# Attention unit and sine layer: the own term moved into the exponentials' diagonal, row sums by feature, values projected first, sine added in PSUM

## The reference

```python
# part 1: heads of 64, causal mask, 2 x 16 heads, n = 1024
attn = softmax(q @ k.T)                       # masked above the diagonal
out  = attn @ v
adj  = clip(attn + eye(n), 0, 1);  deg = adj.sum(-1)
feats = v
for l in range(2):
    h = feats @ gnn_w[l] + gnn_b[l]
    feats = gelu((adj @ h) / deg + feats)
out = out + feats @ lin_w + lin_b
return layer_norm(out @ Wo, gamma_out)
...
# part 2: hidden of 512 features
hidden = x @ W1 + b1
q = hidden + quantum_phase * w_imag * sin(theta + 0.1 * hidden) * 0.1
return relu(q) @ W2 + b2
```

## Time and profile before

| | before |
|---|---|
| median of 3 runs | 2194.48 us (2192.84 to 2197.96) |
| the profiled execution | 2188.13 us, span 2186.3 us |
| PE / PE weight loads busy | 1659.2 us (76%) / 1028.0 us (47%) |
| DVE / ACT / POOL busy | 1128.1 (52%) / 679.5 (31%) / 785.5 us (36%) |
| attention unit, 28 to 1133 us | PE busy 1045.5 us |
| sine layer, 1165 to 1243 us | PE busy 43.1 us, DVE 73.2 us |

### The profile page before, as it was taken

One profiled execution on the slowest core, in us unless ns is written; L12 is line 12 of the kernel. 1 busy time (PEld: TensorE's weight loads), 2 busy tenths in 40 slices (PEclk: granted clock), 3 DMA queues, 4 the chain that ended last, 5 costly groups with the idle time before them and its releaser, 6 DMA issues. The chain is left out here.

```text
span 2186.3 us, 26512 instructions
## 1 busy us (share of the span) xinstructions
PE 1659.2 (76%) x9289; PEld 1028.0 (47%) x9289; DVE 1128.1 (52%) x2512; ACT 679.5 (31%) x990; POOL 785.5 (36%) x511
## 2 busy tenths in 40 slices
PE   3999999999989999999965576955209464767647
PEld 1555655555655556555642345624106211222437
DVE  4334443443444444444448823557703468999615
ACT  1333334433233333334303321322003154544212
POOL 0444345544244443455400031000152105899424
PEclk9899999999999999999886675977559676899759
DMA  1000000000000000000000000000511211212051
GB/s 42 6 6 6 5 5 5 5 0 5 6 1 5 5 5 5 5 5 0 1 1 11 0 6 3 18 12 2 178 46 33 57 31 57 78 67 78 3 153 67
DMA packets 47610, 55.87 MB, mean 26 GB/s; under 512 B 9296, under 2 KB 35048, under 8 KB 47264
## 3 DMA queue, kind: packets, MB, share of 16 engines
q1 hardware_dynamic: 44624, 48.91, 7.5%
q0 software_dynamic: 2912, 6.02, 0.8%
HBM read 42.75 MB, written 12.15 MB: 25 GB/s over the span
## 5 line engine op out<-in xcount | busy, mean ns | idle before, releaser
L356 POOL TENSOR_TENSOR l0a_acc<-l0a_E 128x1792 f32<-128x1792 f32 x16 | 64.3, 4018 | 448.0 <-ACT l0a_E L428 448.0
L821 DVE SCALAR_TENSOR_TENSOR l0a_scrap<-l0a_ring,main_ident 128x128 f32<-128x128 f32 x256 | 74.5, 291 | 271.7 <-PE l0a_ring L560 267.2
L428 ACT ACTIVATE l0a_E<-l0a_ring 128x1024 f32<-128x1024 f32 x192 | 148.8, 809 | 211.8 <-DVE l0a_scrap L821 210.6
L356 POOL TENSOR_TENSOR l0a_acc<-l0a_acc,l0a_E 128x1536 f32<-128x1536 f32 (+2 forms) x96 | 200.8, 2092 | 21.6 <-ACT l0a_E L428 14.0
L2505 PE MATMUL mx_ysum<-mx_hst,main_ident 128*128 128x512 f32 x256 | 142.6, 693 | 44.0 <-POOL mx_hst L2593 38.5
L2606 POOL TENSOR_TENSOR mx_dBu<-mx_XI,mx_BB 128x1024 f32<-128x1024 f32 x64 | 137.5, 2175 | 88.7 <-DVE mx_XI L2669 88.7
L570 PE MATMUL l0a_agg<-l0a_E,l0a_VH 128*64 128x512 f32 (+3 forms) x768 | 154.5, 510 | 0.0
L570 PE MATMUL l0a_agg<-l0a_E,l0a_F 128*64 128x512 f32 (+3 forms) x768 | 141.3, 496 | 0.0
L2578 ACT ACTIVATE mx_dA<-mx_DT,mx_A 128x512 f32<-128x512 f32 x128 | 87.9, 690 | 98.1 <-DVE mx_hst L2686 98.1
L2505 PEld LDWEIGHTS mx_ysum<-mx_hst,main_ident 128*128 128x128 f32 x256 | 54.1, 220 | 115.9 <-POOL mx_hst L2593 57.5
L162 PE MATMUL n_turned<-main_ident,n_xn 128*128 128x128 f32 x96 | 25.8, 458 | 90.6 <-DVE n_xn L132 90.6
(11 more groups left out here) (483 smaller groups left out, 3701.2 us busy)
## 6 DMA issues: line engine op xcount, KB each, us to landing
mx_BB<-mx_brows SPq DMA_DIRECT2D x32, 512.0 KB, 3.6
me_W<-in_f_w SPq DMA_DIRECT2D x16, 256.0 KB, 9.6
l0a_wp<-in_wqkv SPq DMA_DIRECT2D x16, 192.0 KB, 2.3
moe_Wg<-in_f_wg SPq DMA_DIRECT2D x8, 256.0 KB
moe_Wu<-in_f_wu SPq DMA_DIRECT2D x8, 256.0 KB
moe_Wd<-in_f_wd SPq DMA_DIRECT2D x8, 256.0 KB
moe_Y<-rt_zeros SPq DMA_DIRECT2D x2, 1024.0 KB, 10.3
e_back<-moe_Y SPq DMA_DIRECT2D x8, 256.0 KB, 4.8
```

Source lines behind the costliest of these rows:

```text
L356: pool.tensor_tensor(dst, src, E[:, :, ecol[jt]:ecol[jt] + w], ALU.add).then_inc(acc_done, 1)
L428: act.activation(E[:, :, at:at + n], pair(k % 2)[:, :, 0:n], ACT.Exp).then_inc(exp_done, 1)
L821: dve.scalar_tensor_tensor(scrap[:, :], pair(k % 2)[:, h, 0:P], 1.0, ident[:, :], ALU.mult, ALU.mult, accum_out=eii[:, jt, h:h + 1]).then_ ...
```

## The change

The row sums are no longer 16 products of one column: `row_sums` multiplies 64 columns of ones by E and acc, so each head's sum stands in its 64 feature partitions for 1024 tokens, and ScalarE copies it to `RB` (`keep_sums`). `turn_sums` brings them to the old form by 8 products with `pick2` (two columns). `inverse` takes the reciprocals of RB on VectorE, `attended` multiplies them by U untransposed; both run for unit g - 1 within the score stretch of unit g, and `keep_out` adds the result, so `turn_u` and the product with AO in `mix` go. `set_own` adds (s - e) to the 16 diagonals of E in place, so G and `add_own` go, and the aggregation of F1 waits for it. The values are projected ahead of the row scores instead of between them. ScalarE's FT copies stand behind `gelu1` of the first half and both halves of the values. On VectorE the row maxima come after `out1`. In `tail` 7 of the 8 partial products of the output projection are taken ahead of the last pair (`out_tiles`), all of it into two banks, copied in two pieces. In `l0_ffn` four hidden tiles stay in PSUM; ScalarE writes both the angle and the angle in turns; VectorE takes turns off in five instructions; TensorE adds the sine by a product with a diagonal matrix of the coefficients (`add_sine`), and the relu reads PSUM. Declarations, semaphores and the small phase and coefficient sums are left out below.

```diff
-            def keep_v(u):
-                for c in range(2):
-                    act.wait_ge(vw_ready, u * 2 + (c + 1))
-                    wait(act, t1a_done, u * 2)
-                    v = ring[c][:, :].rearrange("p (a w) -> p a w", w=2 * P)
-                    t = slice(4 * c, 4 * c + 4)
-                    act.activation(VH[:, t, :], v[:, :, 0:P], ACT.Copy).then_inc(v_kept, 1)
-                    act.activation(VW[:, t, :], v[:, :, P:2 * P], ACT.Copy).then_inc(vw_kept, 1)
+            def keep_v(u, c):
+                act.wait_ge(vw_ready, u * 2 + (c + 1))
+                wait(act, t1a_done, u * 2 + (c - 1))
+                v = ring[c][:, :].rearrange("p (a w) -> p a w", w=2 * P)
+                t = slice(4 * c, 4 * c + 4)
+                act.activation(VH[:, t, :], v[:, :, 0:P], ACT.Copy).then_inc(v_kept, 1)
+                act.activation(VW[:, t, :], v[:, :, P:2 * P], ACT.Copy).then_inc(vw_kept, 1)
+
+            def keep_sums(g, c):
+                act.wait_ge(r_ready, g * 2 + (c + 1))
+                act.activation(half(RB, c), (prod, turn)[c][:, :], ACT.Copy).then_inc(r_kept, 1)
+
+            def gelu1(g, c):
+                act.wait_ge(s1_done, g * 2 + (c + 1))
+                act.activation(tiles4(F1, c), heads8(S, c).rearrange("p a w -> p (a w)"), ACT.Gelu).then_inc(gelu1_done, 1)
...
+                        wait(act, at_done, g * 2)
                         act.activation(half(UT, 0), agg[0][:, :], ACT.Copy).then_inc(ut_kept, 1)
+                keep_sums(g, 0)
...
+                if nb is not None:
+                    keep_v(g + 1, 0)
+                gelu1(g, 0)
+                if nb is not None:
+                    keep_v(g + 1, 1)
+                if prev is not None:
+                    keep_ft(g, 0)
+                    keep_ft(g, 1)
+                gelu1(g, 1)
...
+            def row_sums(g, prev, nb, c):
+
+                if c:
+                    if nb is not None:
+                        pe.wait_ge(comp_kept, g + 2)
+                        pe.wait_ge(ft_kept, g * 2 - 2)
+                elif prev is None:
+                    wait(pe, ot_kept, g * 2)
+                else:
+                    pe.wait_ge(s2a_done, g * 2)
+                pe.wait_ge(acc_done, g * 7 + (7 if c else 3))
+                bank = (prod, turn)[c]
+                if c == 0:
+                        pe.matmul(bank[hi(h), 0:P], one[:, :], e_tile(h, 0, 0), start=True, stop=True, skip_group_check=True)
+                    for h in range(2):
+                        mm = pe.matmul(bank[hi(h), P:512], one[:, :], acc[:, h, 0:512 - P], start=True, stop=True,
+                                       skip_group_check=True)
+                    for h in range(2):
+                        mm = pe.matmul(bank[hi(h), :], one[:, :], acc[:, h, 512 - P:SEQ - P], start=True, stop=True,
+                                       skip_group_check=True)
+                mm.then_inc(r_ready, 1)
+
+            def turn_sums(g):
+
+                pe.wait_ge(r_kept, g * 2 + 2)
+                for it in range(ST):
+                    mm = pe.matmul(turn[:, 2 * it:2 * it + 2], RB[:, it * P:(it + 1) * P], pick2[:, :], start=True, stop=True)
+                mm.then_inc(s_ready, 1)
...
                 attend(g, 7)
                 product1(g, 0)
+                turn_sums(g)
                 if nb is not None:
-                    row_scores(u, 0, 1)
-                product1(g, 1)
-                if nb is not None:
-                    row_scores(u, 2)
+                    values(u, nb)
                 if prev is not None:
-                    if nb is not None:
-                        pe.wait_ge(comp_kept, u + 1)
+                    pe.wait_ge(s_read, g + 1)
                     turn_f(g, 0)
                 if nb is not None:
-                    row_scores(u, 3)
+                    row_scores(u, 0)
+                product1(g, 1)
+                if prev is not None:
+                    turn_f(g, 1)
+                if nb is not None:
+                    row_scores(u, 1)
                 if prev is not None:
                     pe.wait_ge(s1a_done, g * 2 + 2)
                     mix(g, 0)
-                    turn_f(g, 1)
-                if nb is not None:
-                    values(u, nb)
+                pe.wait_ge(gelu1_done, g * 2 + 1)
+                pe.wait_ge(own_set, g * 16 + 16)
+                for jt in range(4):
+                    mm = aggregate(F1, jt, 0)
+                    if jt == 1 and nb is not None:
+                        row_scores(u, 2)
+                mm.then_inc(agg2_ready, 1)
                 if prev is not None:
                     mix(g, 1)
-                pe.wait_ge(gelu1_done, g * 2 + 1)
-                for jt in range(4):
-                    aggregate(F1, jt, 0, False)
-                turn_u(g, prev, 0)
-                if nb is not None:
-                    row_scores(u, 4)
-                add_own(g, 0)
                 for jt in range(ST):
+                    if nb is not None and jt in (0, 1, 2, 4, 5):
+                        row_scores(u, {0: 3, 1: 4, 2: 5, 4: 6, 5: 7}[jt])
                     if jt == 4:
                         pe.wait_ge(gelu1_done, g * 2 + 2)
+                    mm = aggregate(F1, jt, 1)
+                    if jt == 1:
                         product2(g, prev, 0)
-                    aggregate(F1, jt, 1, False)
-                    if jt == 1:
-                        turn_u(g, prev, 1)
-                    if nb is not None and jt in (1, 3, 4):
-                        row_scores(u, {1: 5, 3: 6, 4: 7}[jt])
+                mm.then_inc(agg2_ready, 1)
                 if nb is not None:
                     max_rows(u)
-                add_own(g, 1)
+                product2(g, prev, 1)
...
+                b = n // PAIRS - 1
+                pe.wait_ge(u2_kept, n * 2)
+                pe.wait_ge(ot_kept, n * 2 - 2)
+                out_tiles(b, n, 0, PAIRS - 1, 0, 1)
                 turn_f(n, 0)
+                out_tiles(b, n, 0, PAIRS - 1, 2, 3)
                 pe.wait_ge(s2a_done, n * 2)
                 mix(n, 0)
                 turn_f(n, 1)
+                out_tiles(b, n, 0, PAIRS - 1, 4, 5)
                 mix(n, 1)
+                out_tiles(b, n, 0, PAIRS - 1, 6, 7)
...
+            def inverse(n, *tiles):
+                for it in tiles:
+                    t = slice(it * P, (it + 1) * P)
+                    dve.reciprocal(AT[:, t], RB[:, t]).then_inc(inv_done, 1)
+
+            def attended(n, c):
+                dve.wait_ge(inv_done, n * ST - (4 - 4 * c))
+                dve.tensor_tensor(half(AT, c), half(AT, c), half(UT, c), ALU.mult).then_inc(at_done, 1)
+
+            def set_own(g):
+                for jt in range(ST):
+                    for h in range(2):
+                        k = 2 * jt + h
+                        dve.scalar_tensor_tensor(e_tile(h, jt, jt), ident[:, :], small[:, 2, k:k + 1], e_tile(h, jt, jt),
+                                                 ALU.mult, ALU.add).then_inc(own_set, 1)
...
+                if prev is not None:
+                    inverse(g, 0, 1)
                 for jt in range(1, ST):
                     own_score(g, jt)
+                    if prev is not None:
+                        inverse(g, *{1: (2, 3), 2: (4, 5), 3: (6,), 4: (7,)}.get(jt, ()))
+                        if jt in (3, 5):
+                            attended(g, (jt - 3) // 2)
                 u = g + 1
                 more = nb is not None
                 if more:
                     keep_q_lo(u)
+                    keep_k_lo(u)
                 sums(g)
-                if more:
-                    keep_k_lo(u)
                 dve.wait_ge(small_ready, u)
                 scaled(S, g, 0, p1_ready, s1a_done)
+                set_own(g)
+                out1(g, 0)
+                scaled(S, g, 1, p1_ready, s1a_done)
+                out1(g, 1)
                 if more:
-                    row_max(u, 0)
-                out1(g, 0)
-                if more:
-                    row_max(u, 1)
-                scaled(S, g, 1, p1_ready, s1a_done)
+                    row_max(u, 0, 1)
+                if prev is not None:
+                    keep_out(g, prev, 0)
                 if more:
                     row_max(u, 2)
-                out1(g, 1)
+                if prev is not None:
+                    keep_out(g, prev, 1)
                 if more:
-                    row_max(u, 3)
-                if prev is not None:
-                    keep_out(g, prev, 0)
-                    keep_out(g, prev, 1)
-                attended(g, 0)
-                if more:
-                    row_max(u, 4)
-                attended(g, 1)
-                if more:
-                    row_max(u, 5, 6)
+                    row_max(u, 3, 4)
...
+            def angle(n):
                 g, c = items[n]
                 act.wait_ge(hid_ready, n + 1)
-                if n >= 3:
```

(42 more changed lines are left out.)

## The result

The changed kernel takes 2235.98 us (2234.87 to 2239.19) against 2194.07 us (2192.84 to 2197.96) of the kernel before, measured side by side: a ratio of 1.019, 95% interval 1.0173 to 1.0208. It is 41.9 us slower. The forecast was 2248 us, with a range of 2165 to 2305. The profiled execution took 2239.19 us around a span of 2237.2.

The account below looks back on a forecast made before the run. The prediction took TensorE's order of work to bound the attention and VectorE the sine layer. Passes +74, output projection -7 and sine layer -13 gave +54 on 2194.5 us: 2248 us, range 2165 to 2305.

Parts of the forecast that it names:

- The chain, with t = 0 at the last piece of scores: Attention pass: set_own beside GpSimd's T delays out1, gelu and the FT copy; TensorE stands still 6.7 us, until 22.0.
- My 19.5: End of out1(g, 0) in us: 18.2 if T's first half falls in, 20.6 if all does; 19.5 taken.
- The two rivals without sharing: set_own does not meet GpSimd: 2150 us if the clock holds, chance 0.18; 2200 us with clock as forecast, chance 0.17.
- The rest of the pass: From TensorE's return to the next third piece of scores 25.1 us, then 19.0; with clock losses the pass is 68.8.
- The new wait of 0.95 at the third piece: TensorE waits 0.95 us at the third piece of scores, since product2(1) no longer stands between scores 1 and 2.
- my sum of 2.7: Clock loss per pass in us: 1.8 for the fall behind the 6.7 us wait, 0.9 for half of a second.
- +74 us for the passes: Attention: each pass grows by 4.8 us, counted for 15.5 passes; range +26 to +102 us.
- Reciprocals: Score stretch: eight reciprocals on VectorE, 0.95 us each, 7.6 a pass, lie in gaps between own scores and cost nothing.
- the rival with 0.12: Reciprocals share the port with GpSimd's sums too: +7 us a pass, 2356 us; chance 0.12.
- Output projection: Batch tail: 56 of 64 products move ahead of the last mixes into waits; -3.4 us a batch, -7 us in all.
- Sine layer: Items take 3.5 to 3.8 us instead of 4.65; fourteen items at -0.95 give -13 us (-23 to +12).

Follow-up runs that it names:

- ft_first: The kernel of split with ScalarE's copy of the first half of FT ahead of the copies of the second value half; 2152.81 us.
- split: Changed kernel with value and FT copies ahead of both gelu1, and the last eight corrections moved behind the fifth row maximum; 2148.1 us, ratio 0.9778.

## Why the prediction was right, step by step

**The chain, with t = 0 at the last piece of scores, was right.** The sums are ready at 9.2 (9.6), the corrections start at 11.0 (11.5), out1(0) ends at 19.2 (19.5), TensorE goes on at 21.5 (22.0) after 6.90 us (6.7). The two terms on which it rests were measured apart: the corrections 4.29 us alone (4.3 taken, 0.27 each), and 3.3 us more beside T. My 19.5 was a choice between 18.2 and 20.6, since no row told how turns are given; that it came within 0.3 us is in part luck. The trace now tells. The sixteen corrections, one by one:

```profile
507.33 0.68 DVE L868 SCALAR_TENSOR_TENSOR l0a_E<-main_ident,l0a_small,l0a_E 128x128 f32<-128x128 f32 x1
507.93 1.43 DVE L868 SCALAR_TENSOR_TENSOR l0a_E<-main_ident,l0a_small,l0a_E 128x128 f32<-128x128 f32 x1
509.29 1.13 DVE L868 SCALAR_TENSOR_TENSOR l0a_E<-main_ident,l0a_small,l0a_E 128x128 f32<-128x128 f32 x1
510.34 1.42 DVE L868 SCALAR_TENSOR_TENSOR l0a_E<-main_ident,l0a_small,l0a_E 128x128 f32<-128x128 f32 x1
511.68 0.34 DVE L868 SCALAR_TENSOR_TENSOR l0a_E<-main_ident,l0a_small,l0a_E 128x128 f32<-128x128 f32 x1
```

Here the engines take turns by the instruction: each of the first four corrections ends about 0.15 us after one of T's four operations, and the other twelve, with GpSimd at rest, follow at 0.26 us. Four in 4.35 us instead of 1.05 is the 3.3.

The Trainium skill, SBUF — State Buffer, section Terms, has the loser of the port block fully; the traces agree, with 7.58 us beside T, 7.29 beside F1B and VB, and 4.29 beside nothing. The two rivals without sharing had 0.35 between them, and they fell.

**The rest of the pass.** From TensorE's return to the third piece of scores I had 25.1 us and 2.7 for the clock, 27.8; it is 28.1 (517.78 to 545.89), and from there to the next last piece 18.7 (19.0). The new wait of 0.95 at the third piece is there, 0.94 us. The wait before max_rows shrank from 1.31 to 0.5 us and no fall follows it. So the clock falls once a pass, not twice, but for 2.8 us of loss instead of 1.8: my sum of 2.7 was right by luck, through two errors that cancel. The steady pass is 68.3 against 68.8.

**The term that was too large is +74 us for the passes.** I took +4.8 us for 15.5 passes; the traces give +58.9. The ten steady intervals went from 64.0 to 68.1, +4.15 each: 6.5 us less than forecast. The first two of each batch grew by 3.4 on average: 5.6 less. The two eighth units grew by 2.0 and 4.6 and the start shrank by 2.8, so the 1.5 further passes of my count are worth 3.8 us and not 7.2. Most of the miss is thus the growth of a pass, and only 3.4 us is the count. Why the first passes of a batch grow less no run shows.

**Reciprocals.** 0.89 to 0.95 us each and never longer, though GpSimd's sums run beside them: the rival with 0.12 is out. They are hidden (the time is 1.7 us shorter without them). `attended` takes 2.2 us instead of 0.69 for its second half, as the prediction had it wait for GpSimd, and the own score behind it costs nothing. What the prediction didn't say is how full the gaps are by then: doubled, they cost 3.4 us a pass.

**Output projection.** Forecast -3.4 a batch; the tails are 4.7 and 4.8 us shorter, -9.5 in all. The early products by themselves are worth 9.2 and 11.1 a batch, as their kernel showed, and part of that only makes up for the eight reciprocals in the tail, behind which TensorE waits 5.68 us without them.

**Sine layer.** Forecast -13, and measured -8.4 and -8.0. The item is faster than I said, 2.97 us by VectorE (3.5 to 3.8), since the clock is 0.86 in the stage and TensorE's products are not the limit. What I left out is a wait. `add(g)` stands in VectorE's order one item after `down(g)` in TensorE's, ahead of the next item's reduction, and `down` is 32 halves, 3.7 us, behind the item's own products. VectorE waits for it four times:

```profile
DVE main_x L1091 <- PE l0f_outp L1109: 20.0, 4, 7.1
```

```profile
1234.81 0.42 DVE L1069 TENSOR_SCALAR l0f_m<-l0f_m 128x512 f32<-128x512 f32 x1
...
1242.72 0.69 DVE L1091 TENSOR_TENSOR main_x<-l0f_outp,main_x 128x512 f32<-128x512 f32 x1 [4.85 <-PE l0f_outp L1109]
```

Before, the combination of the item before stood there (L1048) and an addition at the same place, 1192.48, waited for nothing. By the windows VectorE has 24.1 us less work in the layer (55.7 instead of 79.8), and it is idle for 24.6 us instead of 8.8: of the 20.0 us of these waits only 3.7, at the layer's end, were there before. Placing the addition one item later might help; it wasn't tried.

**The sum.** +74 - 7 - 13 = +54 against 58.9 - 9.5 - 8.4 = +41.0 by the traces, with +0.4 for the rest of the attention +41.4, and 41.9 by the medians. The sign and the mechanism are those forecast. The size was 12 us too large: the passes gave 15 less than forecast and the sine layer 5 less of a gain, and the projection gained 2.5 more than forecast. What the untouched layers do, above, is not in this sum.

## What to carry to other kernels

A block that is moved to save one engine's work has to be priced where it lands: who is queued behind it on its engine, who is queued behind that on the next one, and what the other user of its port does meanwhile. Here some 10 us of TensorE's work a pass were taken out and 4 put in, for corrections on VectorE that take 4.3 us alone and 7.6 where they stood, and the whole change lost 42 us or won 46 by the order of the same instructions. When a steady pass is multiplied, read the first and last passes by their own rows, and divide a stretch that holds both a cost and a gain by a mark between them: here the stretch between the batches shows -2.7 us and holds +2.0 and -4.7.

## What the runs showed of the hardware

- The cost of sharing did not grow with the number of instructions on VectorE: beside T's four operations sixteen corrections took 3.3 us over their own 4.29, and eight (in ft_first) 5.47 us, again 3.3 over their 2.15. One correction went through per GpSimd operation, as the rows above show, and GpSimd's own work was hardly stretched (4.68 us for 4.6).

```profile
478.99 5.47 DVE L870 SCALAR_TENSOR_TENSOR l0a_E<-main_ident,l0a_small,l0a_E 128x128 f32<-128x128 f32 x8
```

- It goes the other way too: GpSimd's 128x512 addition with a broadcast row took 1.26 us alone and 1.71 beside out1. A reciprocal with one SBUF operand was never held, 0.95 us at most beside GpSimd's sums.
- In split, two waits of TensorE of about a microsecond each left the granted clock at 1.00, in ft_first one of 2.0 us was followed by 0.50 in some passes. The total of idle time is the same; in these two kernels the short pieces cost less.
